# A decoder's experts: dispatch as three bf16 products of an exact three-way split, in place of one fp32 product

## What is computed

```python
x = x + _L1_ffn_ref(_layernorm(x, axis=-1), router_w, router_b, w_c_fc, b_c_fc, w_gate, b_gate, w_c_proj, b_c_proj)

# in _L1_ffn_ref, for each sequence: 8 experts, 2 chosen per token, 38 places per expert
top_k_logits, expert_indices = jax.lax.top_k(x @ router_w + router_b, 2)
expert_probs = softmax(top_k_logits)
expert_inputs = zeros((8, 38, 128)).at[expert, place].add(x)      # dispatch
h = einp @ w_c_fc[e] + b_c_fc[e]
g = einp @ w_gate[e] + b_gate[e]
o = silu(h * g) @ w_c_proj[e] + b_c_proj[e]
out[token] = sum(expert_probs * o[expert, place])                 # combine
```

## Time and profile before

| | |
|---|---|
| median of 3 runs | 2346.51 us (2341.09 to 2348.45) |
| profiled execution | 2346.61 us, span 2344.9 us |
| mean granted TensorE clock over the span | 0.880 |
| busy over the span | TensorE 78%, VectorE 74%, ScalarE 64%, GpSimd 53% |
| experts' stage | from 1757 us to the end; first dispatch at 1777, first step at 1787, then turns of some 69.7 us |

### The profile page before, as it was taken

One profiled execution on the slowest core, in us unless ns is written; L12 is line 12 of the kernel. 1 busy time (PEld: TensorE's weight loads), 2 busy tenths in 40 slices (PEclk: granted clock), 3 DMA queues, 4 the chain that ended last, 5 costly groups with the idle time before them and its releaser, 6 DMA issues. The chain is left out here.

```text
span 2344.9 us, 51133 instructions
## 1 busy us (share of the span) xinstructions
PE 1839.0 (78%) x16174; PEld 1342.2 (57%) x16174; DVE 1731.1 (74%) x4035; ACT 1496.6 (64%) x2635; POOL 1236.2 (53%) x1186
## 2 busy tenths in 40 slices
PE   3777777699999944544477569999967999999998
PEld 2555555366666622222245447777755777777776
DVE  4899996588888849999566547888866656665653
ACT  1788888377777735555365648777744666666665
POOL 2556666488888837788576537888850000000000
PEclk9899999699999955555587869999997999999999
DMA  5000000110100030000000000000000000000000
GB/s 141 2 1 0 0 0 2 30 34 22 32 22 22 15 108 1 0 0 0 1 1 0 0 15 10 8 5 8 1 1 1 10 9 0 9 9 9 9 9 10
DMA packets 63116, 32.46 MB, mean 14 GB/s; under 512 B 27736, under 2 KB 59568, under 8 KB 63024
## 3 DMA queue, kind: packets, MB, share of 16 engines
q1 hardware_dynamic: 60576, 30.42, 4.9%
q10 hardware_dynamic: 2448, 0.90, 0.2%
HBM read 27.12 MB, written 4.19 MB: 13 GB/s over the span
## 5 line engine op out<-in xcount | busy, mean ns | idle before, releaser
L3189 DVE SCALAR_TENSOR_TENSOR m_z<-psum,bias_col,m_hb 128x304 f32<-128x304 f32 x256 | 135.1, 532 | 145.1 <-ACT m_hb L3034 133.9
L182 POOL TENSOR_SCALAR mln_ve<-mln_mv 128x4 f32<-128x4 f32 x16 | 3.8, 238 | 432.9 <-DVE mln_mv L160 432.9
L3034 ACT ACTIVATE m_hb<-psum,bias_col 128x304 f32<-128x304 f32 x256 | 131.3, 513 | 140.3 <-PE psum L2930 137.4
L2933 PE MATMUL psum<-m_xt,w_gate 128*128 128x304 f32 x512 | 174.3, 422 | 7.6 <-DVE m_z L3189 7.2
L1412 POOL TENSOR_TENSOR x_gated<-x_score,x_gate 128x1232 f32<-128x1232 f32 x64 | 168.6, 2635 | 13.4 <-ACT x_score L1347 10.4
L2930 PE MATMUL psum<-m_xt,w_fc 128*128 128x304 f32 x512 | 174.2, 422 | 0.6 <-ACT m_xt L3026 0.6
L2942 PE MATMUL psum<-m_hid,w_proj 128*128 128x304 f32 x512 | 170.2, 419 | 0.0
L1354 ACT COPY x_pT<-psum 77x512 f32<-77x512 f32 x256 | 136.3, 582 | 46.0 <-PE psum L1225 44.4
L470 POOL TENSOR_SCALAR_AFFINE_SELECT a_prob<-a_prob 128x1024 f32<-128x1024 f32 x128 | 137.8, 1099 | 51.6 <-ACT a_prob L515 51.0
L1419 POOL TENSOR_TENSOR x_gated<-x_gated,x_rden 128x1232 f32<-128x1232 f32 x64 | 143.9, 2249 | 36.0 <-DVE x_rden L1498 30.9
L509 ACT ACTIVATE a_prob<-psum 128x1024 f32<-128x1024 f32 x128 | 129.5, 1030 | 45.7 <-PE psum L619 29.0
(11 more groups left out here) (407 smaller groups left out, 5637.3 us busy)
## 6 DMA issues: line engine op xcount, KB each, us to landing
x_ctx<-in_ctx_dram SPq DMA_DIRECT2D x32, 154.0 KB
x_mask<-in_mask_BxSxS_ik_dram SPq DMA_DIRECT2D x64, 77.0 KB, 2.6
x_resident<-in_x_dram SPq DMA_DIRECT2D x8, 512.0 KB, 7.1
out_dram<-x_resident SPq DMA_DIRECT2D x8, 512.0 KB, 3.2
x_gate<-in_fside_BxSxS_dram SPq DMA_DIRECT2D x16, 154.0 KB, 2.5
w_fc<-in_L_ffn_w_c_fc_dram SPq DMA_DIRECT2D x1, 2048.0 KB, 9.2
w_gate<-in_L_ffn_w_gate_dram SPq DMA_DIRECT2D x1, 2048.0 KB, 14.4
const<-in_const_dram SPq DMA_DIRECT2D x1, 607.0 KB, 6.5
```

The source lines that it names most:

```text
L2933: pe.matmul(psum[:, 4 + k % 2, 0:N * K], core.w_gate[:, e, f * P:(f + 1) * P], rhs, start=True, stop=True).then_inc(sem["g_ps"], PER_STEP)
L3034: act.activation(hb[:, k % 2, :], psum[:, 2 + k % 2, 0:N * K], ACT.Identity, bias=bias[:, fcb + k:fcb + k + 1]).then_inc(sem["h"], PER_STEP)
L3189: dve.scalar_tensor_tensor(out=z[:, k % 2, :], in0=psum[:, 4 + k % 2, 0:N * K], scalar=bias[:, gb + k:gb + k + 1], in1=hb[:, k % 2, :], op ...
```

## The change

`disp` becomes bf16 (its values are 0 and 1). GpSimd splits the normalised rows of a batch into three bf16 parts whose sum is the fp32 value: it rounds xn to bf16 (a product with ones), subtracts, rounds the rest, subtracts, rounds what is left. These are five instructions over all eight sequences (128 x 1024), linked by a semaphore one behind the other. They start when the batch's xn is written and the dispatches of the batch before are done. In `dispatch`, TensorE waits for the split as well, and makes three bf16 products into the same PSUM bank in place of one fp32 product. `whole` is the tile of ones [128, 128], repeated eight times by its access pattern.

```diff
-        disp = core.sb("m_disp", [P, 2, SLOTS])
+        disp = core.sb("m_disp", [P, 2, SLOTS], BF16)
+        thirds = core.sb("m_thirds", [P, 3, N, C], BF16)
+        rest = core.sb("m_rest", [P, N, C])
+        cut = Chain(core, "m_cut", STEP)
...
                 pe.wait_ge(sem["h"] if n < 2 else sem["xt"], i + (0 if n < 2 else BATCH * (n - 1)))
-                pe.matmul(psum[:, 2 + n % 2, 0:SLOTS], xn[:, n, :], disp[:, n % 2, :], start=True,
-                          stop=True).then_inc(sem["xt_ps"], BATCH)
+                pe.wait_ge(cut.sem, i + (STEP - 1))
+                for k in range(3):
+                    ins = pe.matmul(psum[:, 2 + n % 2, 0:SLOTS], thirds[:, k, n, :], disp[:, n % 2, :], start=(k == 0),
+                                    stop=(k == 2))
+                ins.then_inc(sem["xt_ps"], BATCH)
...
         @block.gpsimd
         def _(pool):
+            whole = bc(core.ones[:], 1, N)
+
+            def split(i):
+                cut.start(i)
+                pool.wait_ge(sem["xn"], i + STEP)
+                pool.wait_ge(sem["xt_ps"], i)
+                cut.link(pool, pool.tensor_tensor(thirds[:, 0], xn[:], whole, ALU.mult))
+                cut.link(pool, pool.tensor_tensor(rest[:], xn[:], thirds[:, 0], ALU.subtract))
+                cut.link(pool, pool.tensor_tensor(thirds[:, 1], rest[:], whole, ALU.mult))
+                cut.link(pool, pool.tensor_tensor(rest[:], rest[:], thirds[:, 1], ALU.subtract))
+                cut.last(pool, pool.tensor_tensor(thirds[:, 2], rest[:], whole, ALU.mult))
+
             pool.memset(comb[:, :, SLOTS:], 0.0)
             pool.memset(o_all[:, N * SLOTS:], 0.0).then_inc(sem["padded"], 1)
             with pool.Fori(1, core.loop_end, STEP) as i:
                 for s in range(STREAMS):
                     ln.rsqrt(pool, i, s)
+                split(i)
```

## The result

| | before | after |
|---|---|---|
| median of 5 runs each | 2343.19 us (2341.09 to 2348.45) | 2384.20 us (2378.38 to 2389.77) |
| profiled execution | 2346.61 us, span 2344.9 | 2389.77 us, span 2388.1 |
| mean granted clock over the span | 0.880 | 0.864 |

The ratio is 1.0166, 95% interval 1.0147 to 1.0184: 34 to 43 us more. The forecast was 2383 us, 36 more than before.

What follows compares the result with a forecast made beforehand. TensorE was taken to bound the experts' loop, busy 68.3 of 69.7 us per turn. Seven turns of 4.1 + 1.2 - 0.6 plus 3.1 in the prologue added 36 us to 2346.6: 2383 us, range 2358 to 2396.

Steps and rivals of the forecast that it cites:

- place and chain: Before step 8, three m_comb instructions wait out GpSimd's split; m_z comes 5.8 us late, overrunning 1.7 us of slack.
- stop: Before the gate product of step 10, TensorE stands still 4.1 us per turn, waiting for m_z of step 8.
- clock: After each turn's TensorE standstill, a stretch at half the granted clock costs 1.2 us, bounds 0 and 1.6.
- products: In the turn's tail, three bf16 products replace one fp32 dispatch product: 0.12 us saved each, 0.6 us per turn.
- prologue: First batch: its split delays both m_oh and the first dispatch 4.1 us, dispatches return 1.0: net 3.1 us lost.
- sum, seven turns and the prologue: Whole kernel: 7 x (4.1 + 1.2 - 0.6) + 3.1 = 36 us more, 2383 us.
- 3.1 us of half speed cost up to 1.6: Per turn: a low-clock stretch seen earlier, 1739.3 to 1742.4 at the least, set the upper bound of 1.6 us.
- five effective dispatches: In the tail, only dispatches 2, 3, 4, 6 and 7 save time; savings in 0, 1 and 5 are waited away.
- The estimate worked out from it: Dispatch products at the skill's price, 26 ns more each: only 0.04 us saved per dispatch; the forecast did not adopt it.
- Vector slips in between: Rival: before step 8 VectorE waits one GpSimd instruction fewer, 1.9 us of stall, 22.7 us more, 2369 us; chance 0.20.
- The split hidden: Rival: VectorE keeps its pace beside GpSimd, only the products count, 5 us fewer, 2341 us; chance 0.12.
- second stall: In each turn: the forecast expected none; one was the example of something worse, chance 0.06.

Runs made afterwards that it cites:

- e1: The changed kernel's split on GpSimd, its parts unused, with the fp32 dispatch product of the kernel before: 2397.25 us, ratio 1.0217.
- e2: The changed kernel's three bf16 dispatch products without a split, the parts zeroed once by GpSimd: 2344.78 us, ratio 0.9985.
- e4: The changed kernel, but from the second batch on each split instruction waits until one more m_comb is done: 2343.01 us, ratio 0.9987.
- e6: The changed kernel plus 16 unused fp32 products on TensorE before the gate product of step 10, in the seven whole turns: 2373.42 us, ratio 1.0117.
- e3: The changed kernel with its split cut into ten GpSimd instructions of 128x512 in place of five of 128x1024: 2348.69 us, ratio 1.0015.
- e5: The kernel before, with its fp32 dispatch, plus one tiny GpSimd operation and five fills that only write SBUF, no split: 2365.50 us, ratio 1.0084.
- e7: The changed kernel with GpSimd's split instructions spread behind m_comb and the first batch's split made by VectorE: 2341.68 us, ratio 0.9981.

## Why the prediction was right, step by step

**The forecast's place and chain were right.** The waits in three m_comb instructions before step 8, m_z behind them, the gate product of step 10, one stop per turn, none before step 12: each is in the timeline of after. e1 puts the whole loss on the split, e2 takes the products out of it, e4 takes the coincidence away and the loss goes.

**Term by term, per turn and in us:**

| term | forecast | measured | from |
|---|---|---|---|
| stop | +4.1 | +4.18 | e6's turn less e4's, 73.03 − 68.85 |
| clock | +1.2, bounds 0 and 1.6 | +2.16 | after's turn less e6's, 75.19 − 73.03 |
| products | −0.6 | −0.84 | e4's turn less before's |
| prologue, once | +3.1 | +3.3 | marks, 36.40 − 33.07 |
| sum, seven turns and the prologue | +36 | +41.8 | medians differ by 41.0 |

The absolute time was hit more closely (2384 to 2383) than the difference was (41 to 36), because the kernel before ran 3 us faster beside the change than in the execution that the sum was made against. That closeness is luck.

**The clock was mis-sized, beyond its bounds.** The step "3.1 us of half speed cost up to 1.6" took the length of one low stretch before as the most that could follow a stop. The trace before gave that length as at the least; after shows 3.4 and 6.8 us, one in every turn. Of the long one 1.7 us lie in the stop (2112.5 to 2114.18, when the gate product starts, the line below), where nothing is lost; half of the other 5.1 is 2.55, half of 3.4 is 1.7, and the mean of the two is 2.1, with 2.16 measured. e6 shows the cause and not only the size: with TensorE busy in the same stop, the stretches are gone. Stops of 0.78 (e3) and 1.82 us (e5) brought none in the turns of their profiles.

```profile
2114.18 1.38 PE L2939 MATMUL psum<-m_xt,w_gate 128*128 128x304 f32 x2 [3.90 <-DVE m_z L3208]
```

**The products saved more.** A dispatch costs 0.12 us less, as the 0.055 us per 128 columns of the earlier trace rows gave it. But five effective dispatches were too few: the waits behind dispatches 0, 1 and 5 grew by 0.12 to 0.13 us, and three dispatches had saved 0.36. From dispatch 0 to the fifth combining product it is 8.30 us after (2155.98 to 2164.28), 8.79 before (2122.76 to 2131.55). So 0.11 of what was to be waited away is kept. And the last two dispatches, with what lies around them, gave 0.36 and not 0.24: 4.85 us from the fifth combining product to the next turn's first step (2131.55 to 2136.40), 4.49 after (2164.28 to 2168.77). The Trainium skill gives a dearer price for such a stream, some 81 ns per product of 128 columns (TensorE: Matmul & The Clock Gate, Back-to-back issue gap). The estimate worked out from it makes the dispatch 0.47 us; it is 0.39 here, so the trace does not bear it out.

**The prologue came out by two errors that cancel.** The first dispatch is 3.4 us late, not 4.1: the split is 11.7 us long, not 12, and only one m_oh waited and not both, since the first (1775.71) got in ahead of the fifth split instruction (1775.72). So close an order can fall either way: in e4 both got in. The dispatches then give 1.2 back (9.98 us from the first to the first step before, 8.82 after; 1.0 was forecast). That leaves 2.3 late at the first step, and the marks say 3.3: the first four products of the steps still run at the half clock (1.02 us apart, 0.51 before).

**The rivals.** "Vector slips in between" did not happen: the order at the start was 2181.59 for GpSimd and 2181.88 for VectorE, and in each gap of the chain the next GpSimd instruction came in behind one instruction of VectorE. "The split hidden" did not happen in the change, but e4 shows that it was right about GpSimd's idle time: 14 us fit in a turn if they keep away from m_comb. Nor was there a second stall.

## What to carry to other kernels

An idle engine is not a free one: before moving work to GpSimd, list what VectorE issues in that stretch with scalar operations from SBUF or two SBUF operands, and how much slack the first consumer behind them has; here 1.7 us of slack met a delay of 5.65. The same change cost 41 us, or gained some 3 (ratio 0.9987), depending on when its GpSimd instructions started (e4), and about nothing with each one half as long (e3): spread them by a semaphore behind the instructions that they would hold up, or cut them short of the slack. And a stop of the bounding engine is to be priced with the half-clock stretch behind it: here 4.2 us of stop brought 2.2 more.

## What the runs showed of the hardware

- Beside a row of GpSimd instructions, VectorE's mostly came one at a time: in e5's back-to-back fills and in the turns of the change, one waiting VectorE instruction got through between two of GpSimd's. It is not a fixed order: in e4's prologue the CAST and both m_oh went by between GpSimd's fourth and fifth.
- A small VectorE instruction of a kind that waits is held up like a large one: m_diff, a difference of two SBUF operands of 128x8, took 0.59 us beside the split (0.17 in e7's and before's prologue) and the CAST of 128x16 1.07 (0.17), while seven MAX8 took 0.56 in both, with GpSimd busy on L3108 from 1771.04 to 1773.38.
- An add of two SBUF operands runs at full pace beside a GpSimd fill (0.47 us in e5), and waits out a GpSimd product that reads two (2.47 us behind L3108).
- VectorE makes the split in 4.7 us for which GpSimd needs 11.7: rounding 128x1024 takes it 0.69 us as a CAST, and GpSimd 2.35 as a product with ones; a CAST on GpSimd was not tried.
